# Transposes of the probabilities ahead of the output products in each step of a cross-attention kernel

## The reference

```
h    = layernorm(x) * gamma + beta            # x: (8, 256, 256)
Q    = h @ Wq;  K = ctx @ Wk;  V = ctx @ Wv   # ctx: (8, 256, 192), 16 heads x 64
attn = softmax(Q @ K^T) * 64 ** -0.5          # per head, 256 x 256
out  = x + (attn @ V) @ Wo + bo
```

## Time and profile before

| | |
|---|---|
| median of 3 runs (lowest, highest) | 373.44 us (373.36, 374.82) |
| the profiled execution: its time, its span | 374.68 us, 372.9 us |
| mean granted TensorE clock | 0.995 |
| busy PE, ACT, DVE, POOL | 356.7, 252.6, 245.6, 161.1 us |
| one ordinary step, from scores to scores | 10.63 us |

### The profile page before, as it was taken

One profiled execution on the slowest core, in us unless ns is written; L12 is line 12 of the kernel. 1 busy time (PEld: TensorE's weight loads), 2 busy tenths in 40 slices (PEclk: granted clock), 3 DMA queues, 4 the chain that ended last, 5 costly groups with the idle time before them and its releaser, 6 DMA issues.

```text
span 372.9 us, 8902 instructions
## 1 busy us (share of the span) xinstructions
PE 356.7 (96%) x3122; PEld 308.4 (83%) x3122; DVE 245.6 (66%) x534; ACT 252.6 (68%) x757; POOL 161.1 (43%) x314
## 2 busy tenths in 40 slices
PE   5896999999999999999999999999999999999984
PEld 4776888988888888888889888889888888988863
DVE  5877576675668656595656866676665956566552
ACT  5776866677766667776667777666776766677761
POOL 6437772445532373332624445324733335333330
PEclk9998999999999999999999999999999999999999
DMA  6940010020002000020000200010000000000000
GB/s 173 262 130 1 5 49 2 0 80 1 2 2 60 20 0 0 0 77 0 0 1 0 77 0 0 0 48 29 0 0 0 28 2 0 3 2 29 3 0 30
DMA packets 10135, 10.39 MB, mean 28 GB/s; under 512 B 864, under 2 KB 9056, under 8 KB 10112
## 3 DMA queue, kind: packets, MB, share of 16 engines
q1 hardware_dynamic: 9728, 9.77, 9.1%
q0 software_dynamic: 112, 0.13, 0.4%
q10 hardware_dynamic: 272, 0.20, 0.2%
HBM read 8.00 MB, written 2.10 MB: 27 GB/s over the span
## 4 chain that ended last, share of the span: by engine, by line
PE 91%; DVE 3%; ACT 3%; POOL 1%; issue 1%; POOLq 0%; DVEq 0%
PE st_ps L705 15%; PE mix_ps L642 15%; PE o_ps L693 13%; PE st_ps L623 13%; PE w_ps L672 12%; PE w_ps L661 11%; PE w_ps L724 10%; ACT prob L381 2%; PE w_ps L606 1%; PE w_ps L598 1%; DVE qk_lo L523 1%; DVE w_lo L442 1%; PE o_ps L593 1%; POOL w_lo L264 1%; DVE neg_max L510 1%
## 5 line engine op out<-in xcount | busy, mean ns | idle before, releaser
L292 POOL TENSOR_SCALAR prob<-prob,inv 128x256 f32<-128x256 f32 x256 | 121.6, 491 | 162.2 <-DVE inv L517 162.2
L381 ACT ACTIVATE prob<-st_ps,neg_max 128x256 f32<-128x256 f32 x256 | 118.6, 474 | 26.4 <-DVE neg_max L510 26.2
L510 DVE TENSOR_REDUCE neg_max<-st_ps 128x2 f32<-128x512 f32 x128 | 82.6, 684 | 35.4 <-PE st_ps L623 35.1
L425 ACT ACTIVATE prob_t<-st_ps 128x512 f32<-128x512 f32 x64 | 38.4, 599 | 49.7 <-PE st_ps L705 49.7
L575 DVE COPY prob_t<-st_ps 128x512 f32<-128x512 f32 x64 | 44.3, 692 | 37.0 <-PE st_ps L705 33.5
L642 PE MATMUL mix_ps<-prob_t,v_sb 128*64 128x256 f32 x512 | 62.3, 385 | 0.1
L705 PE MATMUL st_ps<-ident,prob 128*128 128x128 f32 x512 | 61.8, 274 | 0.0
L705 PEld LDWEIGHTS st_ps<-ident,prob 128*128 128x128 f32 x512 | 57.4, 142 | 0.1
L523 DVE TENSOR_TENSOR qk_lo<-w_ps,qk_hi 128x512 fp32r<-128x512 f32 x64 | 44.0, 688 | 17.6 <-ACT qk_hi L391 17.1
L381 ACT ACTIVATION_READ_ACCUMULATOR prob<-st_ps,neg_max 128x1 f32 x256 | 52.8, 206 | 0.0
L642 PEld LDWEIGHTS mix_ps<-prob_t,v_sb 128*64 128x64 f32 x512 | 34.0, 136 | 18.2 <-issue 0.3
(11 more groups left out here) (70 smaller groups left out, 579.5 us busy)
## 6 DMA issues: line engine op xcount, KB each, us to landing
x_in<-in_x_dram SPq DMA_DIRECT2D x8, 256.0 KB, 3.0
out_dram<-y_sb SPq DMA_DIRECT2D x8, 256.0 KB, 2.2
c_in<-in_ctx_dram SPq DMA_DIRECT2D x7, 192.0 KB, 2.9
w_raw<-in_L_xattn_Wo_dram SPq DMA_DIRECT2D x4, 256.0 KB, 7.6
w_raw<-in_L_xattn_Wk_dram SPq DMA_DIRECT2D x4, 128.0 KB, 4.8
w_raw<-in_L_xattn_Wq_dram SPq DMA_DIRECT2D x4, 128.0 KB, 3.3
w_raw<-in_L_xattn_Wv_dram SPq DMA_DIRECT2D x2, 256.0 KB, 7.0
w_raw<-in_L_xattn_Wv_dram SPq DMA_DIRECT2D x4, 128.0 KB, 6.6
```

Of the source, the lines that this page charges most:

```text
L292: last = nc.gpsimd.tensor_scalar(prob[:, e, r, :], prob[:, e, r, :], inv[:, e, r:r + 1], SCALE, ALU.mult, ALU.mult)
L381: last = nc.scalar.activation(prob[:, e, r, :], st_ps[e][:, r * ROWS:(r + 1) * ROWS], ACT.Exp, bias=neg_max[:, e, r:r + 1], accum_out=sums ...
L510: nc.vector.tensor_reduce(neg_max[:, e, :], st_ps[e][:, :].rearrange("p (r j) -> p r j", r=RT), AX, ALU.max, negate=True).then_inc(max_rea ...
```

## The change

In steps 1 to 31 `turn(u)` comes ahead of `output(u-1)` instead of behind it. Both keep their waits and their instructions; no other engine's order changes. In step 0 (where there is no output product) and in step 32 (where there are no transposes) nothing changes.

```diff
                         project(t, a, turns)
+                if 1 <= u < STEPS:
+                    turn(u, turns)
                 if 1 <= u <= STEPS:
                     output(u - 1, turns)
-                if 1 <= u < STEPS:
-                    turn(u, turns)
                 if u == 0:
                     values(0, turns)
```

## The result

The changed kernel takes 388.01 us (median of 4 runs, 387.82 to 388.39) against 373.4 us before (median of 4, 373.36 to 374.82). Ratio 1.0374, 95% interval 1.0351 to 1.0397: slower by 14.6 us. The forecast was 391.7 us, range 384 to 398, slower with 0.95. The profiled execution took 387.82 us with a span of 386.0; its span is 13.1 us above the 372.9 of before. The two differences (14.6 and 13.1) aren't the same quantity, and the reason is in the experiments (e9).

The account below looks back on a forecast made before the run. TensorE's own stream was taken as the bound, busy 356.7 of 372.9 us. Terms of 9.1, 4.8, 4.4, -0.8 and +0.8 us gave +18.3 us, hence 391.7 us against the median 373.44, range 384 to 398.

Parts of the forecast that it names:

- The bound and the mechanism: TensorE's stream is nearly all the time; head 3's 1.04 us of slack is less than the output products' 1.41 us.
- The hand-over: From POOL's end of scaling to TensorE's transposes, restart included: 0.20 us taken, ends 0.06 and 0.30.
- An ordinary step: 16 of steps 3 to 30: values start 0.57 us later, period 11.20 us instead of 10.63.
- The steps with the split of h and with the normalisation: Seven steps with the split lose 0.68 us each, six with the normalisation 0.74 us each.
- Step 1: Transposes fill TensorE's wait for a piece of Wo: -0.8 us with the clock's fall remaining, -1.95 as the other end.
- Step 31: No project here; the mix of step 32 would start 0.8 us later, behind POOL's scaling of heads 2 and 3.
- The sum: All steps together +18.3 us: the profiled 374.68 becomes 393.0, and against the median 373.44 it becomes 391.7 us.
- fall of the clock in the pauses: Rival: clock falls in longer pauses, 402 us for six normalisation steps (chance 0.09), 440 for all 29 (0.02).
- The wait isn't absorbed: Denies the rival that POOL signals some 0.3 us earlier, so the wait is mostly absorbed: 383 us, chance 0.06.
- the slack of an ordinary step: Rival: not slower if head 3 is ready 0.57 us earlier than shown; 371.5 or 372.6 us, chance 0.03.
- The row of waits: Sign: PE at line 705 waits for POOL's prob about 30 to 37 times, some 15 to 20 us in total.
- the row of `w_lo` in step 1: Sign: no wait of TensorE for w_lo at line 693 in step 1 any more.

Follow-up runs that it names:

- e9: Kernel before the change, with twelve transposes of the identity into o_ps ahead of step 1's output products: 373.14 us, ratio 0.9973.
- e1: Changed kernel with head 3's transposes moved back behind the output products, heads 0 to 2 staying ahead: 374.18 us, ratio 0.9992 against the kernel before.
- e5: Changed kernel with head 3's exponential (ACT) and reciprocal (DVE) ahead of qk_hi and qk_lo of a = 0: 378.89 us, ratio 1.0124 against the kernel before.
- e7: Changed kernel with one more scaling on POOL, to a spare tile, ahead of head 3's in every step: 403.45 us, ratio 1.0779 against the kernel before.
- e8: Kernel before the change, with one more scaling on POOL, to a spare tile, ahead of head 3's in every step: 374.12 us, ratio 1.0002.
- e4: Changed kernel with step 1 put back in the order of before, transposes first in steps 2 to 31: 389.55 us, ratio 1.0408 against the kernel before.
- e2: Changed kernel with transposes of heads 2 and 3 moved back behind the output products, heads 0 and 1 ahead: 371.12 us, ratio 0.9902 against the kernel before.

## Why the prediction was right, and which of its terms were off

*The bound and the mechanism: right.* A stream of TensorE without waits, 1.04 us of slack for head 3, 1.41 us of cover taken away. The chain from the start of the scores to the end of head 3's scaling is 57.59 - 49.74 = 7.85 us after as before, the lateness adds up from step to step, and e1, e5, e7 and e8 show from four sides that the loss is this wait.

*The hand-over: mis-sized.* I took 0.20 us beyond running starts. POOL's end to the first transpose is 0.05. The output products take 59.56 - 58.05 = 1.51 instead of 1.41, but that is hardly a restart behind the wait: in e5, where nothing waits, they take 193.59 - 192.10 = 1.49 behind the transposes, so 0.08 of it belongs to the place and not to the wait. The values in turn need 60.80 - 59.56 = 1.24 instead of 1.32 when they come behind the output products and not behind transposes. All in: 0.05 + 0.10 - 0.08 = 0.07, near the lower bound of 0.06. An ordinary step loses 0.43 to 0.46 us, not 0.57. POOL's row at 29.53 had suggested more.

*The steps with the split of h and with the normalisation:* 0.56 each on the average instead of 0.68 and 0.74, mostly by the same 0.13; in the step with the normalisation that I read, POOL is also through 8.25 instead of 8.29 us behind the scores, since the maxima start 0.03 us earlier. By the starts of the scores the 29 steps 2 to 30 cost 14.4 instead of 18.3 us.

*Step 1: the size was at its other end.* I expected the clock's fall to remain and took -0.8; from scores to scores it was -2.15, of which 1.6 is the clock (e4). The premise, that TensorE's clock would fall in this stretch of transposes with gaps, was wrong here; see below.

*Step 31:* +0.84, expected +0.8.

*The sum:* 14.4 - 2.15 + 0.84 = 13.1 us, as between the spans, against 18.3. The step from there to the median had no ground: I moved the whole sum down by 1.24 us without asking what that difference was. It is the fallen clock of step 1, which the profiled execution had; the median's time lies in the group at full clock. Against a kernel at full clock step 1 is worth -0.5 us, and 14.4 - 0.5 + 0.8 = 14.7 us, against 14.6 measured. That this shift did little harm is luck: -0.8 for a step whose clock fell both before and after happens to lie near the -0.5 for one at full clock in both.

*The rivals.* No fall of the clock in the pauses: the granted clock is at 9 tenths or more in every one of the 40 slices of the page, mean 1.0. The wait isn't absorbed. And the slack of an ordinary step would have had to be larger by 0.43 us, not 0.57, for the change to do no harm; e5 is such a kernel: it has transposes that wait in step 1, the six steps with the normalisation and step 31, and in none of the other 23 steps from 2 to 30.

*The signs.* The row of waits came 35 times, inside 30 to 37, but with 10.0 us instead of 15 to 20, and TensorE's busy time wasn't unchanged (362.9 against 356.7 us): in the ordinary step shown 0.19 us appear as idle and the other 0.24 of the 0.43 us lost as busy. The chain (7.85 us) and the row of `w_lo` in step 1 came as forecast, and the transposes of ordinary steps wait for head 3 alone.

## What to carry to other kernels

When two blocks of an in-order queue are exchanged, put the slack of the moved block's latest input beside the length of the block that it jumps: here 1.04 against 1.41 us, and 0.4 to 0.6 us lost in each of 29 steps. Such a move needn't be all or nothing: split at the input that is late, the same exchange hides other waits and costs next to nothing (e2, 0.6% faster than before at the same clock). And a result can be two effects of opposite sign, and a median and a profiled execution can differ by an effect that the sum also has as a term; the sum over steps, start to start of one and the same instruction, takes them apart in one view.

## What the runs showed of the hardware

- Transposes helped to keep TensorE's clock up. In step 1 of the changed kernel TensorE did 16 transposes and nothing else from 31.83 to 35.37 us, with 1.44 us shown as idle, and was at 1.00 (2.4 GHz); before, after 2.17 us of idle time, it was at 0.58 in 34 to 37 us, and e9's twelve transposes of the identity held it in 12 of 12 executions where 26 of 46 had lost it. The Trainium skill, page "TensorE: Matmul & The Clock Gate", section "Part 4: PE-mode transpose", says that transposes don't count as activity; e9's fp32 transposes did, and the measurement decides.
- They don't hold it in every case. In step 31 of e7 TensorE did groups of four transposes with idle stretches of 0.48, 0.25, 0.79 and 0.41 us between 385.8 and 390.0 us, and the granted clock was 1.00 in 384 to 388 us and 0.65 in 388 to 391. The changed kernel has the same groups there with 0.48, 0.25, 0.79 and 0.26 us and was at full clock. And one of e1's ten executions, with transposes in the stretch of step 1, had a mean clock of 0.995; it wasn't profiled, so where it fell isn't known.
- Whether the clock falls behind one idle stretch of 2.17 us isn't settled by the program: 26 of 46 executions of the same kernel lost it, at 1.2 to 1.3 us, and e4's profile shows the same stretch and wait with the clock at 1.00.
- What a block of products takes depends on what runs ahead of it, with no wait between. Twelve output products take 1.41 us behind 256-column products and 1.49 behind transposes (e5). Five 512-column products, from their start to that of the next block, take 1.24 us behind 256-column products and 1.32 behind transposes.
